# Sandwich of two layers on one core: gate and up products issued whole, the other chunk's mixer steps between products

## What is computed

```python
x = x + _layernorm(_L0_attn_ref(_layernorm(x), wq, wk, wv, wo))
x = x + _layernorm(_L0_ffn_ref(_layernorm(x), gate_w, up_w, down_w, gate_a, gate_b, up_a, up_b, down_a, down_b))
x = x + _layernorm(_L1_attn_ref(_layernorm(x), Win, bin, ln1_w, ..., Wout, bout))   # the mixer
x = x + _layernorm(_L1_ffn_ref(_layernorm(x), w1, s1, w2, s2, w3, s3))
# feed-forward, both times:
hidden = silu(x @ gate.T) * (x @ up.T)        # 512 -> 1376
out = hidden @ down.T                         # 1376 -> 512
# a mixer layer:
y = silu(layernorm(h, l1w, l1b)); y = sconv(y, ...); h = h + y * scl
y = layernorm(h, l2w, l2b); y = silu(y @ w1.T + b1_) @ w2.T + b2_; h = h + y
```

## Time and profile before

| | us |
|---|---|
| median of 3 runs | 946.32 |
| lowest, highest | 945.8, 947.53 |
| the profiled execution | 946.9 |
| its span in the trace | 944.8 |

### The profile page before, as it was taken

How to read it: one execution, slowest core, us unless ns; L and a number is a source line. 1 busy time by engine, 2 the same in 40 slices (tenths; PEclk the granted TensorE clock), 3 DMA queues, 4 the chain that set the end, 5 groups by cost and what they waited for, 6 DMA issues and landing times.

```text
span 944.8 us, 12426 instructions
## 1 busy us (share of the span) xinstructions
PE 807.5 (85%) x4387; PEld 577.3 (61%) x4387; DVE 557.6 (59%) x1130; ACT 317.5 (34%) x504; POOL 432.7 (46%) x545
## 2 busy tenths in 40 slices
PE   3799588877997887885899898989879999879995
PEld 2578344444544443664688677767567777558884
DVE  4444355655655563699935578698796555581015
ACT  3011034433433444553232243332334342334420
POOL 3232113332222122544555666575768585647542
PEclk9899756868667677898999999999979999979998
DMA  8100552344235220403468634443514132214201
GB/s 281 45 0 5 152 156 68 107 139 130 69 115 156 67 91 1 149 29 124 148 219 255 206 115 137 129 139 113 181 33 134 64 92 55 69 61 117 73 21 44
DMA packets 56942, 101.34 MB, mean 107 GB/s; under 512 B 13617, under 2 KB 17201, under 8 KB 54705
## 3 DMA queue, kind: packets, MB, share of 16 engines
q1 hardware_dynamic: 54576, 83.78, 29.4%
q0 software_dynamic: 2304, 16.78, 4.9%
HBM read 74.58 MB, written 27.00 MB: 108 GB/s over the span
## 4 chain that ended last, share of the span: by engine, by line
PE 53%; DVE 20%; DMA 8%; SPq 6%; POOL 5%; issue 4%; ACT 3%; DVEq 0%; ACTq 0%; POOLq 0%
PE psum L1382 18%; PE psum L1402 10%; PE psum L1205 6%; SPq L514 6%; DMA xt_lo<-turned 5%; PE psum L1303 4%; PE psum L1292 2%; DVE bnst L977 2%; PE psum L1254 2%; DMA turned<-w_lo 2%; PE psum L1438 1%; DVE stage_w L1069 1%; PE psum L1284 1%; DVE hn L1143 1%; DVE x L990 1%
## 5 line engine op out<-in xcount | busy, mean ns | idle before, releaser
L909 DVE TENSOR_REDUCE negmax<-psum 128x2 f32<-128x1024 f32 (+3 forms) x128 | 104.9, 822 | 97.6 <-PE psum L1258 96.8
L1382 PE MATMUL psum<-xt_hi,wgu_hi 128*128 128x512 f32 (+1 forms) x352 | 144.3, 410 | 7.2 <-issue 7.2
L666 POOL TENSOR_TENSOR wgu_lo<-raw,wgu_hi 128x512 fp32r<-128x512 f32 (+1 forms) x88 | 118.4, 1351 | 58.5 <-ACT wgu_hi L796 58.4
L1382 PE MATMUL psum<-xt_hi,wgu_lo 128*128 128x512 f32 (+1 forms) x352 | 142.7, 405 | 0.0
L1382 PE MATMUL psum<-xt_lo,wgu_hi 128*128 128x512 f32 (+1 forms) x352 | 142.0, 403 | 0.0
L736 ACT ACTIVATE probs<-psum 128x1024 f32<-128x1024 f32 (+3 forms) x128 | 88.3, 703 | 139.7 <-PE psum L1292 138.4
L642 POOL TENSOR_SCALAR_AFFINE_SELECT probs<-probs 128x256 f32<-128x256 f32 x128 | 51.7, 407 | 181.5 <-ACT probs L736 181.4
L1048 DVE TENSOR_TENSOR hf<-sg,psum 128x512 f32<-128x512 f32 (+1 forms) x44 | 30.1, 684 | 98.0 <-PE psum L1382 70.7
L1382 PEld LDWEIGHTS psum<-xt_hi,wgu_hi 128*128 128x128 f32 (+1 forms) x352 | 67.2, 191 | 24.2 <-issue 9.0
L1303 PE MATMUL psum<-probs,v 128*32 128x128 f32 (+3 forms) x512 | 67.6, 612 | 13.5 <-POOL probs L642 13.4
L1292 PE MATMUL psum<-w_hi,xt_lo 64*128 64x512 f32 (+3 forms) x256 | 67.3, 525 | 13.5 <-DVE w_lo L906 11.4
(11 more groups left out here) (193 smaller groups left out, 1501.7 us busy)
## 6 DMA issues: line engine op xcount, KB each, us to landing
raw<-full SPq DMA_DIRECT2D x60, 256.0 KB, 2.7
raw<-in_gu_t SPq DMA_DIRECT2D x40, 256.0 KB, 3.9
xt_hi<-turned POOLq DMA_DIRECT2D x8, 1024.0 KB, 5.1
xt_lo<-turned POOLq DMA_DIRECT2D x8, 1024.0 KB, 7.0
stage_w<-in_w SPq DMA_DIRECT2D x30, 256.0 KB, 3.2
full<-stage_w SPq DMA_DIRECT2D x30, 256.0 KB, 2.0
turned<-w_hi SPq DMA_DIRECT2D x56, 128.0 KB, 2.4
turned<-w_lo SPq DMA_DIRECT2D x28, 128.0 KB, 2.4
```

The lines of the kernel that those rows point to most:

```text
L666: nc.gpsimd.tensor_tensor(lo, src, hi.bitcast(F32), ALU.subtract).then_inc(sem("w_lo"), 1)
L909: nc.vector.tensor_reduce(negmax[:, g, i, :], pair_of_banks(e)[:, :, 0:(i + 1) * P], AX_X, ALU.max, negate=True).then_inc(sem("row_max"), 1)
L1382: ins = nc.tensor.matmul(bank[q % 3][0:n, :], (wgu_hi, wgu_lo)[hi_w][:, q % 4, k, 0:n], XT[hi_x][:, k, ch * 512:ch * 512 + 512], start=ite ...
```

## The change

In `main`, parts 1 and 2 of every gate and up product get rank -1 in place of 2. They are ready when the part before them ends, so no other PE event can take the place between two parts of a product: a product is issued whole. Part 0 and the down products keep rank 2.

The list that comes out has its transfers, statistics and conversions in other places too, and four guards go with it, where the order was implied before. `xn` at the start of a chunk now waits for the last `xt` that used its buffer (`xn_free`), `h_zero` waits for the last `turns` (they share scratch), and `turns` and `scales` wait for `side_lo 2`. No instruction's work is added or removed.

```diff
@@ -246,6 +246,11 @@
+        def xn_free(s, tau):
+            if tau % TB >= 2 or s == 0:
+                return ("xt", s, tau - 2)
+            return ("xt", *((0, NT - 1), (2, TB - 1), (1, TB - 1), (1, NT - 1))[2 * s - 2 + tau // TB])
@@ -254,7 +259,7 @@
-                put("ACT", 0.65, "xn", s, tau, after=(("x_rstd", s, tau), ("xt", s, tau - 2)))
+                put("ACT", 0.65, "xn", s, tau, after=(("x_rstd", s, tau), xn_free(s, tau)))
@@ -276,7 +281,7 @@
-            put("DVE", 0.45, "h_zero", ch, after=[("win", TB * ch + j) for j in range(TB)] + [("mixer_in",)], rank=0)
+            put("DVE", 0.45, "h_zero", ch, after=[("win", TB * ch + j) for j in range(TB)] + [("mixer_in",), ("turns", DEPTH - 1, 1)], rank=0)
@@ -309,7 +314,7 @@
         def main(us, *event, after=()):
-            put("PE", us, *event, after=[*after, last_main[0]], rank=2, lag=0.0)
+            put("PE", us, *event, after=[*after, last_main[0]], rank=-1 if event[0] == "gate_up" and event[-1] else 2, lag=0.0)
             last_main[0] = event
@@ -757,8 +762,8 @@
-                    if tau >= 2:
-                        after(act, e, "xt", s, tau - 2)
+                    if s or tau >= 2:
+                        after(act, e, *xn_free(s, tau))
@@ -1106,6 +1111,7 @@
                         after(dve, e, "wo", NT - 1)
+                        after(dve, e, "side_lo", 2)
@@ -1116,10 +1122,12 @@
                     dve.wait_ge(sem("chan_in"), 16)
+                    after(dve, e, "side_lo", 2)
@@
                 elif what == "h_zero":
+                    after(dve, e, "turns", DEPTH - 1, 1)
```

## The result

The changed kernel takes **967.6 us** (median of four runs, 966.7 to 975.3) against 946.1 of the kernel before (four runs, 945.6 to 947.5): a ratio of 1.0243, 95% interval 1.019 to 1.0297. The forecast was 965.5, in a range of 954 to 975. The profiled execution has a span of 965.0 us, against 944.8.

A forecast was written before the change was run, and what follows sets the result against it. PE was taken to bound this half, losing 31 us idle, with DVE waited for in the closing stretches. 14.4 + 7.2 + 1.5 - 4 + 0 = +19.1 on 946.9, less 0.6, gave 965.5 us; range 954 to 975.

The forecast's parts named there:

- First end, +14.4: End of mixer 0: lost cover 13.1, relocated work -3.9, longer chain +5.2; +14.4 us, bounds +6 and +18.
- Cover, +13.1: First end: products and 36 down matmuls that hid under the closing chain now run before its last part; +13.1 us.
- The chain behind it: First closing stretch: DVE work of about 31 us, then the xt to win relay; 36.5 us instead of 31.3, +5.2.
- Second end, +7.2: End of mixer 1: lost cover +5.5 and longer chain +1.7; +7.2 us, bounds +1 and +11.
- Chain +1.7: Second closing stretch: DVE's work and the wait for the first wout, about 32.5 us against 30.9; +1.7.
- The cover of 24 matmuls, 5.5: Second end: of 11.0 us of cover, 24 down matmuls, 5.5 us, are left; +5.5.
- -3.9: First end: four xt and three win of chunk 1 move ahead of the first product, leaving the time behind; -3.9 us.
- Waits beside the mixers, -4: PE waits for hn and sin_in beside both mixers shrink by a third; -4 us; 0 by the SBUF port rule.
- Start of the first layer, 0: First layer's waits for merge, 12.5 us, are a DVE matter and stay; 0, between -3 and +3 us.
- Guards, 0: The added guard waits stand for things long over or relays already counted; 0 us.
- Clock: Longer idle stretches at both ends run wout and transposes at 1.2 GHz; +1.5 us, between 0 and +4.
- The marks I had set: Signs expected in the changed profile: two gaps, mixer idle time, DVE almost solid, last stage unchanged; limits that would refute it.

The follow-up runs named there:

- e3: Changed kernel with products whole only in ffn(1, 1), beside mixer 0, thirds elsewhere; 956.8 us, ratio 1.012 to the kernel before.
- e4: Changed kernel with products whole only in ffn(3, 0), beside mixer 1, thirds elsewhere; 963.5 us, ratio 1.0181 to the kernel before.
- e5: Changed kernel with one cut per product: a mixer step may enter behind the first third, not the second; 955.9 us, ratio 1.0088 to the kernel before.
- e6: Changed kernel with the 36 down matmuls of the last group of ffn(1, 1) held until h_down 0 7 is issued; 977.6 us, ratio 1.0306 to before.
- e8: Changed kernel plus 61 extra matmuls, results unread, in PE's waits in the first closing stretch; 964.7 us, ratio 1.019 to the kernel before.
- e2: Changed kernel with products whole only in ffn(1, 0), beside no mixer, thirds elsewhere; ratio 1.0064 to the kernel before.
- e1: Changed kernel with product priority put back to thirds, leaving only the four guards, every engine's order as before; ratio 1.0051 to the kernel before.
- e9: Changed kernel plus extra matmuls, results unread, in PE's waits in both closing stretches; ratio 1.0162 to the kernel before.
- e10: Changed kernel with products in thirds, order of before, plus extra unread matmuls in the waits of both closing stretches; ratio 1.0029 to the kernel before.

## Why the prediction was right, point by point

**The mechanism.** Whole products make the mixer later than its cover, and both ends pay. e3 and e4 show it one end at a time, e5 in between. I had put it as 13.1 us of products and down matmuls "done before the chain's last part starts"; that agrees with mixer 0 itself, which needs 12.9 us longer (117.6 instead of 104.7), and e6 got nothing back by moving 36 of these matmuls. That a step has to wait for the end of a product explains all of it at mixer 1 and 4.7 us of it at mixer 0. For the rest there the rival is DVE's other work beside mixer 0, and no run holds it fixed.

**First end, +14.4.** Cover, +13.1: the order held to it, but the stretch grew by 19.1. Of the 6.0 us above the cover 3.0 are more waiting (12.1 us instead of 9.1) and 3.0 more busy time, at a mean clock of 0.96 instead of 0.99. The chain behind it was counted at 36.5 us from DVE's work, "together about 31 us, nearly without a gap". It was 39.4, and for another reason than DVE: DVE was busy for 27.4 us in it and idle for 12.0. Without the fall of the clock it is 33.4 (e8). So the count was 3.1 us too long, and the clock, which stood in a term of its own with +1.5 for both ends, costs up to 6.0 at this one alone; 3.5 us of that are the transposes and `win` of chunk 1, counted at 4.9 us and measured at 8.4 (4.8 in e8). Two errors of the sum against each other. Both stretches together grew by 27.2 us, where the terms for them make 18.3.

**Second end, +7.2.** Chain +1.7, measured +1.6. The cover of 24 matmuls, 5.5: its stretch came out at -2.5 where -3.9 and +5.5 make +1.6. Of the 4.1 us between, 1.3 are less waiting (109.4 - 106.3 = 3.1 idle against 112.0 - 107.6 = 4.4 in the earlier trace rows); the other 2.8 are in busy time, in part the first product: nine matmuls ran at the lower clock behind 697.82 us, three behind 719.76.

**Waits beside the mixers, -4.** Wrong. Idle time beside mixer 0 rose from 9.1 to 12.1 us, beside mixer 1 it fell by 1.3: +1.7 together. The waits that I expected to be shortened by the wider raster (`hn`, `sin_in`) came to 3.3 and 3.4 us beside mixer 0, where they had been 2.8 and 3.0, and a new one stood in the last down group, for POOL's `h_lo` (2.9 us), because `full` on DVE came late. Of the two values that I set side by side, 0 was the nearer. The durations of `h_norm` do go with POOL's work: before, it took 0.42 us in nine of 18 cases and 1.3 to 1.5 us in the other nine, all of them while POOL was at work. In the changed kernel only five of 18 were long, and still the waits did not shrink; these durations alone do not set them. The wait list beside mixer 0:

```profile
PE psum L1427 <- DVE sin_in L1175: 3.4, 2, 2.1
PE psum L1417 <- DVE hn L1151: 3.3, 2, 2.8
PE psum L1410 <- POOL h_lo L676: 2.9, 1, 2.9
```

**Start of the first layer, 0.** Wrong by -3.7, just outside the ±3 I gave it. With `merged 3` behind a product the wait of 8.2 us for it is gone, and 5.8 us for POOL's `wgu_lo` ahead of that product and 3.0 us for `merged 4` stand in its place. But e2 shows that this is not kept: there it was given back beside mixer 0. In the sum it happened to stand where my -4 for the waits stood.

**Guards, 0.** By their waits, yes. By the result of e1 they come with 0.5%, some 3 us of slower matmuls in the profile.

**Clock.** The sentence on which I put the rule of the Trainium skill (page TensorE: Matmul & The Clock Gate, section What's actually happening: throttled by default, activity releases it) took the number of restarts as the only thing that counts, and the term as near 0. The rows disagree with what I drew from it: in a stretch of short bursts between waits PE is at 1.2 GHz for most of the time (0.59 mean), and this, up to 6.0 us at the first end, is as large as the miss beside mixer 0. The rule itself, that activity releases the clock, fits e8.

The marks I had set: first gap "about 35", 41.2; second "about 27", 26.6; idle time beside the mixers "some 9", 15.2; last stage unchanged, 0.9 shorter; DVE "almost solid", not so. I had written that the prediction is wrong if that idle time grows or if the first layer moves by more than 3 us. Both happened. That 965.5 and 967.6 lie so close is luck in good part. The first end, the largest term, came out 8.9 us above its terms; against it stand the 3.7 us of the first layer, the 4.1 beside mixer 1, the 0.9 of the last stage and the 1.6 by which the attention, which the change does not touch, happened to be shorter. What was right is the direction, the two places and the cause of the greater part. (946.9 + 19.1 - 0.6 is 965.4, not 965.5; nothing hangs on it.)

## What to carry to other kernels

Where a long thin chain runs between pieces of bulk work on one engine, a step that is ready may have to wait for the end of a piece: here the chain of some 105 us grew by 5 us at 2 us pieces and by 13 us at 3 us pieces, and pieces below 1 us made it 1.3 us shorter and the kernel no faster. Look at what the other engines do between the steps too; more than half of the 13 us lay there. A filler that is held back for the end of the chain helps only if the chain isn't the late one; ask first which of the two the other waits for. Gains ahead of such a chain are not gains until they have been seen behind it.

## What the hardware showed unexpectedly

- The clock can fall behind a short wait or not at all behind the same one: after 1.2 us of waiting `win` took 1.81 us in e1 and 1.09 us before. Two kernels with the same order on every engine, one with guards that never waited, lay 3 us apart by such places. A fall costs nothing in the end where a wait behind it takes the loss up, as before at 626.99 us.
- e8 and e9 are one program up to `h_down 0 7`; beside mixer 0 they took 137.1 and 141.7 us, at a granted clock of 0.98 and 0.94. So a difference of up to 4.6 us in that stretch can be read only together with its clock.
- 20 matmuls of no use in a 5.2 us wait cost nothing (`h_turn` had 0.31 us left to wait), and with 41 more in the waits behind them they gave 6.0 of the 39 us back; where the stretch was covered anyway (e10), the same trick gave 1.9 us in all.
- The same DVE instruction (`h_norm`, 128x256) takes 0.42 us or 1.3 to 1.5 us, with nothing between; all 14 long cases in two kernels overlap with work of POOL, though not every overlap makes one long.
